# Attention heads: who counts the 256-column tile, and how ranks are compared with the number taken

## What is computed

```python
draft = jnp.einsum('bhqd,bhkd->bhqk', qr, kr)        # 32 heads of 16, 1024 x 1024
draft = draft + jnp.where(causal_future, neg, 0.0)
_, draft_indices = jax.lax.top_k(draft, 128)          # num_remain = max(min(S, 128), S - int(S * 0.9))
mask = mask.at[b_idx, h_idx, s_idx, draft_indices].set(0.0)
mask = jnp.where(causal_future, neg, mask)
scores = jnp.einsum('bhqd,bhkd->bhqk', qr, kr) / 4 + mask
out = jnp.einsum('bhqk,bhkd->bhqd', jax.nn.softmax(scores), v)
```

## Time and profile before

| | |
|---|---|
| median of 3 runs (lowest, highest) | 3204.84 us (3202.18, 3208.5) |
| span of the profiled execution | 3199.0 us |
| attention heads, from the first row maximum to the last tile | about 2069 to 3044 us |
| busy in the whole span: PE, DVE, ACT, POOL | 90%, 77%, 62%, 52% |

### The profile page before, as it was taken

The page is one execution under the profiler, slowest core; times in us unless marked ns, Lnnn a source line. Parts: engine busy times, 40 slices in busy tenths (PEclk is TensorE's granted clock), DMA queues, the critical chain, the costliest instruction groups (busy, mean ns, idle before and its releaser), DMA issues. The chain is left out here.

```text
span 3199.0 us, 50581 instructions
## 1 busy us (share of the span) xinstructions
PE 2877.9 (90%) x15823; PEld 1746.2 (55%) x15929; DVE 2459.9 (77%) x4628; ACT 1981.7 (62%) x4218; POOL 1649.3 (52%) x3659
## 2 busy tenths in 40 slices
PE   8899999999999999999999989748887888888779
PEld 4455455454464554554554644526666666666654
DVE  5677687696696786876976976858888888888746
ACT  2464554564564555545645523679999999999823
POOL 3236245264273362452542644777777777777503
PEclk9999999999999999999999999859889988988889
DMA  2222222232132231221321310000000000000010
GB/s 89 66 78 95 73 93 81 71 116 82 66 112 75 74 111 66 89 89 66 104 74 60 119 48 27 2 1 2 2 2 2 2 2 2 2 2 2 1 51 27
DMA packets 65804, 169.63 MB, mean 53 GB/s; under 512 B 11776, under 2 KB 19328, under 8 KB 64512
## 3 DMA queue, kind: packets, MB, share of 16 engines
q1 hardware_dynamic: 54448, 115.17, 11.0%
q10 hardware_dynamic: 11088, 51.19, 4.6%
HBM read 161.08 MB, written 5.24 MB: 52 GB/s over the span
## 5 line engine op out<-in xcount | busy, mean ns | idle before, releaser
L2059 ACT ACTIVATE X<-ah_z,ah_trial 128x256 bf16<-128x256 f32 (+6 forms) x896 | 733.1, 825 | 23.9 <-POOL ah_trial L2162 14.3
L1207 ACT ACTIVATE m_mix<-m_mix,m_cs 128x128 f32<-128x128 f32 x1024 | 312.9, 388 | 254.9 <-DMA m_mix<-cs_rows 254.8
L2012 PE MATMUL ah_ps_o<-a_v,X 128*128 128x17 f32 x2304 | 318.9, 265 | 0.2 <-DVE hT L2270 0.2
L2012 PEld LDWEIGHTS ah_ps_o<-a_v,X 128*128 128x128 f32 x2304 | 303.3, 200 | 0.3 <-issue 0.3
L1089 POOL TENSOR_TENSOR m_xdec<-m_xdt,m_decay_out 128x512 f32<-128x512 f32 x112 | 140.0, 1250 | 213.1 <-DVE m_xdt L1333 202.1
L1117 POOL TENSOR_TENSOR m_squares<-m_squares 128x256 f32<-128x256 f32 x128 | 107.4, 839 | 274.1 <-ACT m_squares L1219 274.1
L2252 DVE MAX8 ah_top<-ah_ps_m 128x8 f32<-128x256 f32 (+6 forms) x224 | 186.0, 830 | 71.4 <-PE ah_ps_m L1962 66.6
L1013 PE MATMUL m_ps_d<-m_w_out,m_gate 128*128 128x512 f32 x512 | 235.2, 602 | 0.0
L1013 PE MATMUL m_ps_x<-m_w_out,m_gate 128*128 128x512 f32 x512 | 233.9, 600 | 0.0
L2070 ACT ACTIVATE X<-ah_ps_e 128x512 f32<-128x512 f32 (+3 forms) x384 | 185.0, 483 | 53.6 <-PE ah_ps_e L1999 44.9
L2231 DVE TENSOR_SCALAR_CACHE_REDUCE X<-ah_z,ah_cut 128x256 bf16<-128x256 f32 (+6 forms) x224 | 193.3, 874 | 26.5 <-POOL ah_cut L2167 26.5
(11 more groups left out here) (319 smaller groups left out, 7556.6 us busy)
## 6 DMA issues: line engine op xcount, KB each, us to landing
m_mix<-cs_rows SPq DMA_DIRECT2D x128, 512.0 KB, 4.3
m_w_proj<-in_w_proj ACTq DMA_DIRECT2D x69, 512.0 KB, 3.3
m_fade<-fade_rows SPq DMA_DIRECT2D x224, 128.0 KB, 2.9
m_w_out<-in_w_out ACTq DMA_DIRECT2D x7, 2048.0 KB, 7.7
X<-in_x SPq DMA_DIRECT2D x8, 256.0 KB, 5.9
m_w_out<-in_w_out SPq DMA_DIRECT2D x1, 2048.0 KB, 10.3
x_away<-X SPq DMA_DIRECT2D x1, 2048.0 KB, 7.3
X<-x_away SPq DMA_DIRECT2D x8, 256.0 KB, 6.2
```

Source lines behind the costliest of these rows:

```text
L1207: act.activation(mix[:, u % 3, h, :], mix[:, u % 3, h, :], ACT.Relu, bias=cs[:, c, h0 + h:h0 + h + 1], scale=-1.0).then_inc(lag_done, 1)
L2012: last = pe.matmul(ps_o[:, t, :], eT[:, g % 3, b * P:(b + 1) * P], v[:, b0 + b, h // REP, :], start=i == 0 and b == 0, stop=b0 + b == t, s ...
L2059: act.activation(sign[:, at % 2, 0:(t + 1) * P], z[:, h % RING, cols(t)], ACT.Sign, bias=trial[:, h % RING, 0, t - 1:t], scale=-1.0, accum ...
```

## The change

Of the four sweeps of a head, the first and the third leave out tile 1 on ScalarE. VectorE counts it there (`count_low`): one comparison of the tile in `z` with `trial`, summed from -128 into `lower`; GpSimd doubles it into `signs` ahead of the move. The rank compare takes two tiles in one operation (1 and 2, 3 and 4, 5 and 6; 7 alone), with `ranks` now holding 128 minus the rank, and stands behind MAX8 of the odd tile.

```diff
+    ON_VECTOR = ((0, 0), (1, 2))
@@ count, ScalarE
-                if t == 1 and k == 0:
+                if t == scalar_tiles(k)[0]:
...
-                        if live(n - back):
+                        if live(n - back) and t in scalar_tiles(k):
                             count(n - back, k, t)
@@ move, GpSimd
+                if (h, k) in VECTOR_AT:
+                    pool.wait_ge(counted_low, VECTOR_AT[h, k] + 1)
+                    pool.tensor_scalar(signs[:, r, 0:1], lower[:, r:r + 1], 2.0, None, ALU.mult).then_inc(own, 1)
+                    at += 1
+                    pool.wait_ge(own, at)
@@ excess, VectorE
-                dve.tensor_scalar(surplus[:, at % 2], ranks[:], taken_count[:, h, t - 1:t], float(TOPK), ALU.add,
-                                  ALU.is_ge).then_inc(pick_step, 1)
+                to = min(t + 2, NT)
...
+                dve.tensor_tensor(surplus[:, t - 1:to - 1], taken_count[:, h, t - 1:to - 1].unsqueeze(2).to_broadcast([P, to - t, 8]),
+                                  ranks[:].unsqueeze(1).to_broadcast([P, to - t, 8]), ALU.is_ge).then_inc(excess_done, 1)
+            def count_low(h, k):
+                at = VECTOR_AT[h, k]
+                if k == 0:
+                    dve.wait_ge(guessed, h + 1)
+                    dve.wait_ge(z_done, h * NT + 2)
+                else:
+                    dve.wait_ge(moved, MOVE_AT[h, k - 1] + 1)
...
+                dve.tensor_scalar(below[:], z[:, h % RING, cols(1)], trial[:, h % RING, 0, 0:1], -float(P), ALU.is_lt, ALU.add,
+                                  accum_out=lower[:, h % RING:h % RING + 1]).then_inc(counted_low, 1)
@@ pick, VectorE
-                if t == 1:
-                    excess(h, t)
                 dve.wait_ge(marked, at + 1)
                 dve.max(top[:, r], ps_m[:, m_at(t):m_at(t) + (t + 1) * P]).then_inc(pick_step, 1)
-                dve.wait_ge(pick_step, 3 * at + 2)
-                dve.copy_predicated(top[:, r], surplus[:, r], taken8[:]).then_inc(pick_step, 1)
-                if t < W:
-                    excess(h, t + 1)
+                if t % 2:
+                    excess(h, t)
+                dve.wait_ge(excess_done, h * (NT // 2) + (t + 1) // 2)
+                dve.wait_ge(pick_step, 2 * at + 1)
+                dve.copy_predicated(top[:, r], surplus[:, t - 1], taken8[:]).then_inc(pick_step, 1)
@@ VectorE's loop
+                if live(n - 1):
+                    count_low(n - 1, 2)
                 if live(n - 4):
                     divide(n - 4)
...
                 for t in range(1, NT):
+                    if t == 4 and live(n + 1):
+                        count_low(n + 1, 0)
                     if live(n - 2):
                         pick(n - 2, t)
@@ constants
-            "ranks8": np.arange(8, dtype=np.float32),
+            "ranks8": TOPK - np.arange(8, dtype=np.float32),
```

More of the change, by code:

```diff
@@ L1838, in attention_heads_fast @@
     MOVE_AT = {hk: i for i, hk in enumerate(order)}
+    scalar_tiles = lambda k: range(2 if k in [q for _, q in ON_VECTOR] else 1, NT)
+    SCALAR_AT = {hkt: i for i, hkt in enumerate((h, k, t) for h, k in order for t in scalar_tiles(k))}
+    VECTOR_AT = {hk: i for i, hk in enumerate(hk for hk in order if hk[1] in [q for _, q in ON_VECTOR])}
     sign_share = np.cumsum([0] + [t + 1 for _ in SWEEPS for t in range(1, NT)])
@@ L1862, in attention_heads_fast @@
         signs = sb("signs", [P, RING, W])
+        lower = sb("lower", [P, RING])
+        below = sb("below", [P, 2 * P], BF16)
         side = sb("side", [P, 3, W])
@@ L1873, in attention_heads_fast @@
         top = sb("top", [P, 2, 8])
-        surplus = sb("surplus", [P, 2, 8], I32)
+        surplus = sb("surplus", [P, W, 8], I32)
         ranks = sb("ranks", [P, 8])
@@ L1895, in attention_heads_fast @@
             sem("s_done"), sem("z_done"), sem("sampled"), sem("stats_done"), sem("guessed"))
-        counted, moved, cut_done, own = sem("counted"), sem("moved"), sem("cut_done"), sem("own")
+        counted, counted_low, excess_done = sem("counted"), sem("counted_low"), sem("excess_done")
+        moved, cut_done, own = sem("moved"), sem("cut_done"), sem("own")
         take_done, marked, pick_step, pick_done, least_done = (
@@ L2048, in count @@
             def count(h, k, t):
-                if t == 1 and k == 0:
-                    act.wait_ge(guessed, h + 1)
-                elif t == 1:
-                    act.wait_ge(moved, MOVE_AT[h, k - 1] + 1)
+                if t == scalar_tiles(k)[0]:
+                    if k == 0:
+                        act.wait_ge(guessed, h + 1)
+                    else:
+                        act.wait_ge(moved, MOVE_AT[h, k - 1] + 1)
                 if k == 0:
                     act.wait_ge(z_done, h * NT + t + 1)
-                at = MOVE_AT[h, k] * W + t - 1
+                at = SCALAR_AT[h, k, t]
                 if at >= 2:
@@ L2130, in move @@
                 at, r = steps[0], h % RING
-                pool.wait_ge(counted, (MOVE_AT[h, k] + 1) * W)
+                if (h, k) in VECTOR_AT:
[3 more added lines that the diff above has]
+                    pool.wait_ge(own, at)
+                pool.wait_ge(counted, SCALAR_AT[h, k, NT - 1] + 1)
                 pool.tensor_tensor(trial[:, r, 1], signs[:, r], table[:, 2], ALU.subtract).then_inc(own, 1)
@@ L2234, in excess @@
             def excess(h, t):
[L2236 to L2239, removed]
-                dve.tensor_scalar(surplus[:, at % 2], ranks[:], taken_count[:, h, t - 1:t], float(TOPK), ALU.add,
-                                  ALU.is_ge).then_inc(pick_step, 1)
+                to = min(t + 2, NT)
+                if h:
+                    dve.wait_ge(pick_step, 2 * h * W)
+                dve.wait_ge(take_done, h * W + to - 1)
+                dve.tensor_tensor(surplus[:, t - 1:to - 1], taken_count[:, h, t - 1:to - 1].unsqueeze(2).to_broadcast([P, to - t, 8]),
+                                  ranks[:].unsqueeze(1).to_broadcast([P, to - t, 8]), ALU.is_ge).then_inc(excess_done, 1)
+            def count_low(h, k):
+                at = VECTOR_AT[h, k]
+                if k == 0:
+                    dve.wait_ge(guessed, h + 1)
+                    dve.wait_ge(z_done, h * NT + 2)
+                else:
+                    dve.wait_ge(moved, MOVE_AT[h, k - 1] + 1)
+                if at:
+                    dve.wait_ge(counted_low, at)
+                dve.tensor_scalar(below[:], z[:, h % RING, cols(1)], trial[:, h % RING, 0, 0:1], -float(P), ALU.is_lt, ALU.add,
+                                  accum_out=lower[:, h % RING:h % RING + 1]).then_inc(counted_low, 1)
             def pick(h, t):
@@ L2248, in pick @@
                     dve.wait_ge(pick_done, at - 1)
-                if t == 1:
-                    excess(h, t)
                 dve.wait_ge(marked, at + 1)
                 dve.max(top[:, r], ps_m[:, m_at(t):m_at(t) + (t + 1) * P]).then_inc(pick_step, 1)
-                dve.wait_ge(pick_step, 3 * at + 2)
-                dve.copy_predicated(top[:, r], surplus[:, r], taken8[:]).then_inc(pick_step, 1)
-                if t < W:
-                    excess(h, t + 1)
+                if t % 2:
[3 more added lines that the diff above has]
+                dve.copy_predicated(top[:, r], surplus[:, t - 1], taken8[:]).then_inc(pick_step, 1)
                 if h >= 2:
                     dve.wait_ge(et_done, (h - 2) * NCH + LAST_CHUNK[t] + 1)
-                dve.wait_ge(pick_step, 3 * at + 3)
+                dve.wait_ge(pick_step, 2 * at + 2)
                 dve.match_replace(picked[:, h % 2, cols(t)], top[:, r], ps_m[:, m_at(t):m_at(t) + (t + 1) * P],
@@ L2387, in constants @@
     return {"masks": masks, "small": small, "cos": np.cos(angle), "sin": np.sin(angle) * sign,
-            "cut_table": cut_table.astype(np.float32), "ranks8": np.arange(8, dtype=np.float32),
+            "cut_table": cut_table.astype(np.float32), "ranks8": TOPK - np.arange(8, dtype=np.float32),
             "ranks": -np.arange(1, NH + 1, dtype=np.float32)}
```

## The result

The changed kernel takes 3241.98 us (median of 4 runs, 3235.55 to 3244.62), the kernel before 3204.69 us (4 runs, 3202.18 to 3208.5): a ratio of 1.0116, 95% interval 1.0104 to 1.0128. The change costs 37.3 us. The forecast was 3227 us: right in sign, too small by 15, and the time lies 1 us above the upper end of the range.

What follows compares the result with a forecast made beforehand. The prediction took VectorE's loop with TensorE, not ScalarE, to bound the heads. A count (0.39) and paired compares (0.45) add 0.84 us a pass, +21.8 us in 26 passes, giving 3227 us, range 3203 to 3241.

Steps and rivals of the forecast that it cites:

- The bound: In the heads, VectorE's loop with TensorE sets the pass; ScalarE, 96% busy, rides along, so removing its counts costs 0.
- 1.1 + 1.8: ScalarE's idle time in a pass: about 1.1 us before the change, forecast to grow by about 1.8 (0.98 + 0.84).
- GpSimd's first move: First update of the cut in a pass; part of ScalarE's added idle time was expected to be spent waiting for it.
- The count at the seam, cost nothing: VectorE's new count before the reciprocal: 0.39 us, hidden in a 0.57 us wait, so cost 0.
- The reciprocal's wait: VectorE's wait at the seam, forecast to shrink from about 0.6 to 0.2 us or less.
- The compares, 3 x 0.15: Paired compares push back the copies after MAX8 of tiles 3, 5 and 7: 0.45 us a pass, bounds 0.30 and 0.93.
- Copy to load: From predicated copy to match load, about 0.3 us for all tiles; taking the compare out gives back nothing.
- the compares were on the path: Rival, chance 0.15: removed single compares in VectorE's tight stretch cost 0.23 us each; net +0.16 us a pass, 3209 us.
- the second count at 0.39 us a pass: VectorE's count before MAX8 of tile 4, where nothing is waited for: 0.39 us a pass, bounds 0.39 and 0.47.
- the sum that left the clock to a rival: VectorE's added work per pass, 0.39 + 0.45 = 0.84 us, times 26 passes is +21.8 us, with no clock term.
- the short passes vanish: Rival, chance 0.20: TensorE's added idle time prolongs the low clock, all passes become long ones, +32 us, 3237 us.
- Start and end of the heads, even: Filling and draining the pipe: ScalarE's saving and GpSimd's extra 0.3 us stand against each other, -2 to +1 us.

Runs made afterwards that it cites:

- two kernels with TensorE kept busy: Fourteen matmuls of 256 columns a pass, never read, put at TensorE's seam waits: in the kernel before 3171.74 us, in the changed kernel 3190.91 us.
- kernels of the table above: Seven kernels: before, compares alone 3221.97, seam count alone 3203.63, count at tile 3 3222.46, tile 4 count alone 3236.49, both counts 3232.78, after 3241.98 us.

## Why the prediction was right or wrong

**The bound: right.** ScalarE's 96% was not the bound. Leaving its counts out with no replacement changed nothing, and the idle time of 3.0 us a pass is near the 1.1 + 1.8 that was forecast. None of it is spent on GpSimd's first move, where a part was expected.

**The count at the seam, cost nothing: right.** Alone it measures 0. The reciprocal's wait fell to 0.18 us as forecast, though in the changed kernel only in its short passes.

**The compares, 3 x 0.15: near in sum by luck, wrong in mechanism.** The forecast had the copies of tiles 3, 5 and 7 pushed back by the compare ahead of them, and those of the others not. From MAX8 to copy tiles 3, 5 and 7 take 0.07 to 0.08 us more, half of the price, while the pair lasts 0.16 us instead of 0.23. But tiles 4 and 6, which have no compare there, take 0.09 and 0.07 more too. The copy now waits on one more semaphore and reads another slice of `surplus`, in all tiles; which of the two costs the time, and whether the compare costs any, was not tried. Five times 0.075 is 0.38, near 0.45. Copy to load stayed at 0.28 on the mean of 26 passes, so nothing came back. That part was forecast, and with it the rival that the compares were on the path falls: an operation in a hand-over was free. The Trainium skill ("VectorE: DVE Perf Modes", "Rules for kernel authors") says to keep the number of operations low; here three fewer, with the rest partly in another place, cost 17.8 us.

**The step that failed: the second count at 0.39 us a pass, and with it the sum that left the clock to a rival.** The count takes 0.40 us, so the price is right as a duration of VectorE. Its cost is not: alone it makes 32.3 us in 26 passes, 1.24 a pass, and in the changed kernel, against the same count one tile earlier, 19.5 us, 0.75 a pass, where 0.39 x 26 = 10.1 was forecast. What the runs show in its place is TensorE's wait behind tile 4, lengthened from 0.88 to 1.36 us, and behind it a second low spell of the clock in every pass.

That spell shows by kinds of passes. A short pass went from 28.75 us (mean of 8 of 25) to 29.44 (7 of 25), the next kind from 29.98 (17) to 30.69 (12): +0.69 and +0.71, near the 0.84 of the sum. That makes 18 us in 26 passes, and 21.8 was forecast. But the sum took the passes to stay of the same kinds. Six of 25 are of a third kind, of 32.08 us, 1.40 above the second, in which the long second spell makes VectorE wait before tile 6: 8.4 us. One short pass fewer gives another 1.2. With 25 x 0.70 = 17.5 that is 27.1, the whole difference of the 25 passes (739.7 and 766.8 us).

The rival "the short passes vanish" has nearly the right time, 3237, for the wrong reason: 7 short passes in 25 remain (8 before), and the loss is a spell at another place. It was given as an alternative of 0.20, where the clock belonged in the sum as a term. Its trace was there to be read: TensorE's wait of 0.88 us behind tile 4 stood in the timeline before, exactly behind the place where 0.40 us was to be added, and in the one pass in which it was 1.31 us the clock fell.

**What else is in the 15 us.** Counted by runs, the count at tile 4 explains 19.5 - 10.1 = 9.4 of them. The other 6 are the compares: alone they cost 17.8 us, where 0.45 x 26 = 11.7 was forecast.

**Start and end of the heads, even: wrong.** They take 34.3 - 28.8 = 5.5 us more of the span, 3.5 of it in the end part. There it is the time up to the last match that grows, by 3.9 us. In the two kernels with TensorE kept busy that time is the same, which speaks for the clock. Those two differ behind the last match, by 3.2 us, and the cause of that is open. Of the start only its size is known. The remaining 3 us of the 37 lie within the spread of the changed kernel's runs, 9 us.

**What stays open:** what makes one pass of a kernel short and the next long. The compares alone lengthen the mean pass by 0.58 us, where the hand-overs from MAX8 to copy of tiles 3 to 7 take some 0.4 more, and the runs do not say why. Nor do they say why a wait of 1.35 us brings the second spell in every pass of the changed kernel, and in half of them with the idle matmuls.

## What to carry to other kernels

Before adding work to an engine that another waits for, look at the wait of the waiting engine behind that very place, and at the clock behind its longest waits: here a count of 0.40 us cost 32 us alone in one place, and in a wait one tile earlier next to nothing. Look also for single passes in the old trace that already do what the change will do: here one pass in 26 had the longer wait, and the low spell behind it. A saving on the busiest engine can be worth nothing; leave the work out without replacement once, and the run says what the saving can bring. When a stretch has a granted clock under 1.00, try to win that back: here it was worth 32 us.

## What the runs showed of the hardware that was not expected

- Fourteen idle matmuls a pass raised the granted clock from 0.90 to 0.99 and took 32 us off, though TensorE was already busy for 82% of the time.
- Lengthening one TensorE wait from 0.88 to 1.28 or 1.36 us brought a second low spell of 4 to 6 us on average, in 22 to 25 passes of 25. In the kernels of the table above it came in no pass with a wait of 0.88 to 1.02 us; in the kernel before and in the one with the count at tile 3 it came once each, behind a single wait of 1.31 and 1.32 us. With the idle matmuls at the seam, where 20 passes of 25 had a wait of 1.35 us or more, it came in 12.
- The order of GpSimd's operations of 0.2 to 1.5 us was worth some 11 us once the clock was high (3171.74 to 3160.48), though GpSimd was busy for only 77% of the time (571.46 of 741 us).
